# Attention's norm, projections and swish inside the first FFN stage, with the order of FFN's bias and low-rank steps changed

## What is computed

```python
x = x + 0.5 * ffn(layernorm(x))     # first FFN, gives x1
x = x + attn(layernorm(x))          # gated slot attention, gives x2
x = x + 0.5 * ffn(layernorm(x))     # second FFN, same weights

def ffn(x):                          # d_ff = 1024 = 16 groups of 64
    mask_logits = einsum('bl,lxy->bxy', x @ m1, m2) + mb
    quant_mask = argmax(mask_logits, axis=-1)      # one of 64 in each of 16 groups
    mid = relu(einsum('ai,aji->aj', x, w1p[j, quant_mask]))
    return einsum('ai,aij->aj', mid, w2p[j, quant_mask]) + b2

def attn(x):
    q = swish(x @ Wq); k = swish(x @ Wk); v = x @ Wv
    f = log_sigmoid(x @ Wf) / 8; s = 1 - exp(f)
    o = recurrence(q, k, v, s, f)                  # over 512 steps, 4 heads
    return (rmsnorm(o) * g) @ Wo
```

## Time and profile before

| | us |
|---|---|
| median of 3 runs (3420.39 to 3427.73) | 3422.68 |
| the profiled execution | 3423.29 |
| its span in the profile | 3421.5 |
| PE busy over the span | 3177.3 (93%) |
| VectorE busy | 2675.9 (78%) |
| ScalarE busy | 1646.5 (48%) |
| GpSimd busy | 1315.3 (38%) |

### The profile page before, as it was taken

How to read it: one execution, slowest core, us unless ns; L and a number is a source line. 1 busy time by engine, 2 the same in 40 slices (tenths; PEclk the granted TensorE clock), 3 DMA queues, 4 the chain that set the end, 5 groups by cost and what they waited for, 6 DMA issues and landing times. The chain is left out here.

```text
span 3421.5 us, 102510 instructions
## 1 busy us (share of the span) xinstructions
PE 3177.3 (93%) x36736; PEld 2711.9 (79%) x36736; DVE 2675.9 (78%) x4369; ACT 1646.5 (48%) x4554; POOL 1315.3 (38%) x2170
## 2 busy tenths in 40 slices
PE   5999999999979999789999999999799999999999
PEld 4888888888866566578888888888588888888888
DVE  7999999999952332287778877887699999999998
ACT  3333333333335565577777777777433333333332
POOL 3333333333324333255555555555333333333332
PEclk9999999999999999899999999999899999999999
DMA  3111111111115555523333333333211111111111
GB/s 84 57 51 55 51 55 52 54 52 53 55 64 199 198 196 197 181 89 102 101 101 101 101 101 101 101 101 101 63 54 55 51 55 51 55 51 55 52 54 46
DMA packets 224965, 290.57 MB, mean 85 GB/s; under 512 B 25460, under 2 KB 191732, under 8 KB 224888
## 3 DMA queue, kind: packets, MB, share of 16 engines
q1 hardware_dynamic: 224888, 289.52, 26.7%
HBM read 171.97 MB, written 117.44 MB: 85 GB/s over the span
## 5 line engine op out<-in xcount | busy, mean ns | idle before, releaser
L578 PE MATMUL mid_ps<-xT_hl,w_hl 128*128 128x128 f16 x12288 | 729.1, 219 | 0.0
L425 PE MATMUL res_ps<-w_hl,midT_hl 128*128 128x256 f16 x6144 | 712.5, 273 | 1.2 <-DVE x_out L546 1.2
L578 PEld LDWEIGHTS mid_ps<-xT_hl,w_hl 128*128 128x128 f16 x12288 | 698.3, 98 | 0.5
L382 POOL TENSOR_TENSOR var_eps<-moments,eps_col 128x1 f32<-128x1 f32 x384 | 110.5, 288 | 1480.5 <-DVE moments L378 1480.5
L425 PEld LDWEIGHTS res_ps<-w_hl,midT_hl 128*128 128x128 f16 x6144 | 589.6, 98 | 65.5 <-DVE midT_hl L533 1.7
L486 ACT ACTIVATE midT_hl<-mid_ps 128x1024 f16<-128x1024 f32 x256 | 262.2, 1024 | 692.4 <-PE mid_ps L589 692.4
L512 DVE TENSOR_TENSOR_SCAN runmax<-restart,logits_ps 128x1024 f32<-128x1024 f32 x256 | 581.2, 2270 | 3.4 <-PE logits_ps L567 3.3
L397 ACT ACTIVATE xn_hl<-xc,rstd 128x256 f16<-128x256 f32 x384 | 194.1, 506 | 434.1 <-POOL rstd L387 349.4
L372 DVE BATCH_NORM_STATS2 stats<-x_in 128x6 f32<-128x256 f32 x384 | 161.6, 421 | 294.6 <-DMA x_in<-x 290.2
L533 DVE SCALAR_TENSOR_TENSOR midT_hl<-mid_ps,midT_hl 128x1024 f16<-128x1024 f32 x256 | 313.4, 1224 | 15.4 <-ACT midT_hl L486 7.5
L517 DVE TENSOR_TENSOR step<-runmax 128x1024 bf16<-128x1024 f32 x256 | 314.6, 1229 | 7.9
(11 more groups left out here) (143 smaller groups left out, 6215.3 us busy)
## 6 DMA issues: line engine op xcount, KB each, us to landing
projected<-qkfv_out SPq DMA_DIRECT2D x128, 512.0 KB, 2.9
qkv<-projected SPq DMA_DIRECT2D x128, 384.0 KB, 3.4
x<-x_out SPq DMA_DIRECT2D x256, 128.0 KB, 1.7
x_in<-x SPq DMA_DIRECT2D x256, 128.0 KB, 2.1
x_res<-x SPq DMA_DIRECT2D x256, 128.0 KB, 2.1
x_in<-in_L_attn_x SPq DMA_DIRECT2D x128, 128.0 KB, 2.0
x_res<-in_L_attn_x SPq DMA_DIRECT2D x128, 128.0 KB, 2.1
gate<-projected SPq DMA_DIRECT2D x128, 128.0 KB, 3.1
```

Source lines behind the costliest of these rows:

```text
L425: last = nc.tensor.matmul(dst, left(lp, k), right(rp, k), start=(k == 0 and lp == rp), stop=(k == blocks - 1 and lp == 1))
L578: nc.tensor.matmul(mid_ps[t.slot][:, cols], w1_hl[:, wp, k, cols], xT_hl[:, t.ring, xp, k], start=(c % PER_BANK == 0 and k == 0 and wp == xp),
```

## The change

The stage `project_phase` is gone. Its work is done by `ffn_phase` when it is called with `projected` (the first call alone):

- `Norm` now owns its tiles. A second one, `norm2`, takes its input from `x_out`, where `finish` has just written x1, in place of an own load from HBM. So the 128 loads of x1 for the projections are gone; the store of x1 stays.
- PE gets `transpose_x1` (tile s-4), `project_qk` and `project_vf` (s-5) between `transpose_x` and `down`. They write into the free half of the bank of `res_ps` and into two single banks, `qk_ps` and `vf_ps`.
- To free those banks, `mid_ps` is single in the first FFN (`MIDS` is 1), so `up` of tile t waits for `mid_low` of tile t-1, not t-2. The second FFN keeps two.
- ScalarE gets `norm2.high` (s-3), `evacuate_x1T` (s-4), `swish` and `scale_vf` (s-5), GpSimd `norm2.centre` (s-2), VectorE `norm2.stats` and `norm2.aggregate` (s-2) and `norm2.low` (s-3), SP the store of the projections (s-6), from a ring of two tiles in place of four.
- New waits: `transpose_x1` of tile t waits for `finish` of tile t+2; `down` of tile t waits for the evacuated x1 of tile t-3; `finish` of tile t for `norm2.centre` of tile t-2.
- In both FFN stages `add_bias` now stands ahead of `centre` in GpSimd's step, and `low_low` ahead of `first_max` in VectorE's.

```diff
-            def load(...):   sp.dma_start(x_in[:, t.slot], src_t[t.row])
+            def load(...):   sp.dma_start(self.x[:, t.slot], src_t[t.row])
...
-            mid_ps = [psum(scope, f"mid_ps{s}_{base}", 2 * BANK) for s in range(2)]
+            mid_ps = [psum(scope, f"mid_ps{s}_{base}", 2 * BANK) for s in range(MIDS)]
...
-                    pipeline(pool, [(lambda t: norm.centre(pool, t), 5), (add_bias, -1)],
+                    stages = [(add_bias, -1), (lambda t: norm.centre(pool, t), 5)]
+                    if projected is not None:
+                        stages += [(lambda t: norm2.centre(pool, t), -2)]
...
+                        stages = [high, (lambda t: norm2.high(act, t), -3), (low_high, 2), (mid_high, 0),
+                                  (evacuate_xT, 3), (evacuate_x1T, -4), (swish, -5), (scale_vf, -5)]
...
-                    pipeline(dve, [(finish, -2), (lambda t: norm.stats(dve, t), 5),
-                                   (first_max, 1), (low_low, 2), (reached, 1),
+                    stages = [(finish, -2), (lambda t: norm.stats(dve, t), 5), (low_low, 2), (first_max, 1),
...
+                        after(pe, mid_low_made, t, lag=MIDS)
...
                     def down(t):
                         after(pe, mid_low_made, t)
                         after(pe, out_made, t, lag=1)
+                        if projected is not None:
+                            after(pe, norm2.xT_made, t, lag=3)
...
-        ffn_phase(a["x"], x1, 0)
-        project_phase(x1, projected)
+        ffn_phase(a["x"], x1, 0, projected)
```

More of the change, by code:

```diff
@@ L433, in ffn_phase @@
             UNROLL, LONGEST_LAG = 8, 4
+            D = d_model
+            MIDS = 1 if projected is not None else 2
             scope = ExitStack()
@@ L463, in store, with store_projected @@
                         sp.dma_start(dst_t[t.row], x_out[:, t.slot]).then_inc(out_stored[t.slot], 16)
-                    pipeline(sp, [(lambda t: norm.load(sp, t, src_t), 6), (load_residual, 0), (store, -2)],
-                             tiles, base, UNROLL, LONGEST_LAG)
+                    def store_projected(t):
+                        after(sp, vf_scaled, t)
+                        sp.dma_start(projected[t.row], qkvf_out[:, t.slot]).then_inc(qkvf_stored[t.slot], 16)
+                    stages = [(lambda t: norm.load(sp, t, src_t), 6), (load_residual, 0), (store, -2)]
+                    if projected is not None:
+                        stages += [(store_projected, -6)]
+                    pipeline(sp, stages, tiles, base, UNROLL, LONGEST_LAG)
+                    if projected is not None:
+                        for s in range(2):
+                            sp.wait_ge(qkvf_stored[s], 16 * tiles // 2)
                     for s in range(2):
@@ L545, in finish @@
                         after_dma(dve, out_stored, t, lag=2)
+                        if projected is not None:
+                            after(dve, norm2.centred, t, lag=2)
                         nc.vector.scalar_tensor_tensor(x_out[:, t.slot],
@@ L548, in finish @@
                                                        x_res[:, t.slot], ALU.mult, ALU.add).then_inc(out_made, 1)
-                    pipeline(dve, [(finish, -2), (lambda t: norm.stats(dve, t), 5),
-                                   (first_max, 1), (low_low, 2), (reached, 1),
-                                   (lambda t: norm.aggregate(dve, t), 5), (lambda t: norm.low(dve, t), 4),
-                                   (reject, 1), (mid_low, 0)],
-                             tiles, base, UNROLL, LONGEST_LAG)
+                    stages = [(finish, -2), (lambda t: norm.stats(dve, t), 5), (low_low, 2), (first_max, 1),
+                              (reached, 1), (lambda t: norm.aggregate(dve, t), 5),
+                              (lambda t: norm.low(dve, t), 4), (reject, 1), (mid_low, 0)]
+                    if projected is not None:
+                        stages = [(finish, -2), (lambda t: norm.stats(dve, t), 5), (low_low, 2),
+                                  (lambda t: norm2.stats(dve, t, out_made), -2), (first_max, 1), (reached, 1),
+                                  (lambda t: norm.aggregate(dve, t), 5), (lambda t: norm2.aggregate(dve, t), -2),
+                                  (lambda t: norm2.low(dve, t), -3), (lambda t: norm.low(dve, t), 4),
+                                  (reject, 1), (mid_low, 0)]
+                    pipeline(dve, stages, tiles, base, UNROLL, LONGEST_LAG)
                 @block.tensor
@@ L714, in project_phase @@
+                    stages = [(mask_logits, 1), (low_rank, 2), (up, 0), (pick, 0), (transpose_x, 3)]
+                    if projected is not None:
+                        stages += [(transpose_x1, -4), (project_qk, -5), (project_vf, -5)]
+                    pipeline(pe, stages + [(down, -1)], tiles, base, UNROLL, LONGEST_LAG)
             scope.close()
```

185 lines of the change are left out of this document (77 added, 108 removed).

## The result

The changed kernel takes 3365.95 us (median of 4 runs, 3364.02 to 3370.86), the kernel before 3422.59 on the same chip: ratio 0.9835, 95% interval 0.9818 to 0.9852. It is faster by 57 us. I had forecast 135 us less: 3288, with a range up to 3320. The sign was right, and more than half of the gain is missing.

A forecast was written before the change was run, and what follows sets the result against it. Bound before: a ring of VectorE and GpSimd, with PE only nearly full. Terms 29 + 29 + 77.7 - 0.6 = 135 us off the 3421.5 us span gave 3286.5, hence 3288 us measured; range 3278 to 3320.

The forecast's parts named there:

- What bounds the kernel: Both FFN stages before the change: PE is only nearly full, and a VectorE-GpSimd ring of 7.49 us keeps the time.
- the FFN step from 7.41 to 7.17: Each FFN stage: the two reorderings leave PE as the bound, saving 29 us in each.
- the ring through `x_res`: FFN step: finish, scan, aggregate, GpSimd's work to x_res, next finish; 7.49 us long, cut by moving the bias.
- That `low_low` had to move as well: VectorE's FFN step: PE's transposes wait for low_low behind the 2.27 us scan; moved ahead, it is done 2 us early.
- A merged step of 10.01 us: First FFN with projections inside: PE needs 7.17 us for the FFN and 2.84 us for a tile's projections and transposes.
- the first rival: Merged step: PE still waits late at new transposes, down or projections; one place 26 us, two 52; chance 0.14.
- the third rival: Merged step: VectorE holds GpSimd off, lengthening the 9.1 us ring to 11.3; 161 us more, 3449 us; chance 0.04.
- 124 x 2.84 us inside the stage: Merged stage: 124 of the 128 projections lie inside FFN steps and cost 352.2 us there.
- Does a merged step stay PE's?: Merged stage: yes, as VectorE's 7.9, ScalarE's 4.4 and GpSimd's 3.8 us a step are all below 10.
- I charge 0.6 us once: 0: Start of the merged stage, no projections between yet: up's wait for the single mid_ps costs 0.6 us once.
- The ring of 9.1 us: Merged step: low_low through aggregates, two centre, norm2.high and low_high back to low_low; tightest new ring, 0.9 us spare.
- The tail, 16.1 us: Behind the first FFN's last down: finish 0.7, last four tiles 11.4, scaling 0.8, store and stage's end 3.2 us.

The follow-up runs named there:

- b_orders: The kernel before with only the two changed orders (bias ahead of centring on GpSimd, low_low ahead of the scan on VectorE) in both FFN stages: 3369.0 us, ratio 0.9843.
- u4_pe: The changed kernel with PE's loop in the merged stage rolled to 4 steps a trip instead of 8: 3295.0 us, ratio 0.9622.
- u4_ring: u4_pe with ScalarE's low_high put first in a merged step, ahead of both high: 3291.2 us, ratio 0.9615.

## Why the prediction was wrong

- **What bounds the kernel; the FFN step from 7.41 to 7.17.** Right. Scans of the second FFN are 7.17 us apart, `finish` no longer waits for `x_res`, and the two FFNs gave 54 us (`b_orders`) where the sum had 58. The reason was half right: the ring through `x_res` was the whole of it. That `low_low` had to move as well was an unneeded part of the argument.
- **A merged step of 10.01 us.** Right as the time of a step in which nobody waits: 7.17 + 2.84 is met to the last digit by the mean step of `u4_pe`, from its ninth on. Late waits, the first rival, didn't come; nor did the third rival, though `rstd` on GpSimd takes 1.30 us in a merged step where it took 0.90.
- **124 x 2.84 us inside the stage.** This is the step that failed. It took the time of one step and multiplied it by the number of steps, as if every step were alike. Twelve times PE's loop jumped back to code that had to be fetched again, and the two steps behind each jump lost 6.3 us together: 75 us. The question was put in the prediction ("Does a merged step stay PE's?") and answered with busy times, rings and buffers. The 28 matmuls that a tile adds were priced by their time, not by the code that they are. 28 x 2 instructions x 8 steps is 448 more in a loop of 1559, and that sum was not made. Nothing in the rows of before shows such a stall, since both loops were held there; the number of instructions in the body was to be had from the kernel itself.
- **The start, "I charge 0.6 us once: 0".** Wrong by its size. Five steps took 44.8 us instead of 35.9. The ring of 9.1 us was compared with a step of 10.01, but at the start the projections don't yet fill the step, and it stands against 7.17; four of the five steps take 9.0 to 9.2. Cutting it (`u4_ring`) brought 4 us. In the changed kernel's timeline ScalarE's `low_high` comes only behind the second `high`:

```profile
77.25 0.61 POOL L395 TENSOR_TENSOR att_xc<-x_out,att_moments 128x256 f32<-128x256 f32 x1
...
77.95 0.51 ACT L404 ACTIVATE att_xn_hl<-att_xc,att_rstd 128x256 f16<-128x256 f32 x1 [0.86 <-POOL att_xc L395]
78.37 0.26 ACT L521 ACTIVATE low_hl<-front_ps 128x128 f16<-128x128 f32 x1
...
78.66 0.29 DVE L589 TENSOR_TENSOR low_hl<-front_ps,low_hl 64x128 f16<-64x128 f32 x1 [1.34 <-ACT low_hl L521]
```

- **The tail, 16.1 us.** Right: the last `down` starts at 1392.33 and its 24 matmuls take 2.62 us, counted as in the prediction; attention's first load is issued at 1410.69, 15.7 us behind that. These rows answer to the earlier trace rows:

```profile
1392.33 2.78 PE L432 MATMUL res_ps<-w_hl,midT_hl 128*128 128x256 f16 x24
...
1410.69 1.76 SPq L807 DMA_DIRECT2D gate<-projected  x4
```

The sum, then: 3286.5 was the span forecast; 75 us for the branches, 8.4 us more at the start and 0.4 less at the end make 3369.5, and the span is 3369.1.

The range missed too. All its rivals were waits between engines, and the largest slower case near the forecast was one late wait a step, 26 us. A range that ends at 3320 says that nothing which the trace of before doesn't show can cost 30 us. The chip gave 3289 for the same work with a smaller loop body, and 3366 with the larger one.

What stays open: the exact bound. A body of 1559 is held at all starts tried but one, and 1769, 2025 and 2335 were refetched at each start tried. By the same estimate a loop that lies across seven blocks is held and one across eight is not, in every run here; no run was made to test it. By this count the zone around 73 would be the 22 places from 66 to 87; its width wasn't tried. Why the body of 1559 at 73 is fetched at every second branch and not at each wasn't settled either. And one thing doesn't fit yet: the merged loop begins at 169 in the same count, so its second stall would put a block's end near 196 and not at 88. Code that this count doesn't hold may lie between the two stages, so places can be compared within a stage only.

## What to carry to other kernels

When an edit puts more instructions into an unrolled loop, count the body of the loop on the engine that bounds, a matmul as two, and compare it with loops of that engine that are known to run freely. If steps come out uneven with the period of the loop, look at the branch's own duration and at the code queue, and halve the unrolling before anything else: a held branch is free here. A ring that a long step covers must also be held against the short steps at the start and the end of the stage.

## What the runs showed of the hardware

- A loop of 1559 instructions on TensorE, a matmul counted as two, runs without new code from trip to trip (branch of 0.21 us), except from one start; a larger one (1769, 2025, 2335) is fetched again on every trip, in packets of 16 KB. The branch then lasts 3.3 to 4.2 us, of which 1.6 to 2.5 us are seen as idle time of the engine ahead of the loop's first matmul; the `down` issued before still runs at its start. This bears out the rule of the Trainium skill named above, that a branch to code no longer held stalls, but neither 2048 instructions, nor its "2-page window" describes what is held: a loop of 6.1 blocks of 256 is, and one of 6.9 isn't.
- The start of the loop counts. Where the merged loop begins in the changed kernel, a second stall of 1.2 to 2.4 us follows 27 instructions behind it and the granted clock falls (to a mean of 0.63 over 4 us), 6.3 us a branch in all; begun 32 instructions later, a branch costs 2.2 us, and the clock falls at one of the twelve alone (0.65 from 360 to 364 us).
- Sixty-four idle instructions ahead of one loop moved an untouched loop, more than 2000 us further on, to a place where it was refetched, for 43.6 us over six pairs of steps. A small edit anywhere ahead can change the time of a large loop in this way, so a difference of one per cent between two versions may be neither's merit.
